# Full attention: heads paired on two halves of the partitions, scores issued a step ahead, maximum chunks set between halves of the value matmuls

## What is computed

```python
scores = jnp.einsum('bhtd,bhsd->bhts', q, k) * scale
attn = jax.nn.softmax(scores.astype(jnp.float32), axis=-1).astype(q.dtype)
y = jnp.einsum('bhts,bhsd->bhtd', attn, v)
```

## Time and profile before

| | |
|---|---|
| median of 3 runs | 7337.34 us (7335.41 to 7339.68) |
| the profiled execution's own time | 7338.15 us |
| its span | 7336.3 us |
| PE / PEld / DVE / ACT / POOL busy | 75 / 43 / 63 / 45 / 36 % of the span |
| maxima chunks reduced (L340) | 1904, from 130.2 to 2612.3 us of the span |
| exponentials (L517) | 896, 796.0 us |

### The profile page before, as it was taken

How to read it: one execution, slowest core, us unless ns; L and a number is a source line. 1 busy time by engine, 2 the same in 40 slices (tenths; PEclk the granted TensorE clock), 3 DMA queues, 4 the chain that set the end, 5 groups by cost and what they waited for, 6 DMA issues and landing times. The chain is left out here.

```text
span 7336.3 us, 228324 instructions
## 1 busy us (share of the span) xinstructions
PE 5478.9 (75%) x94991; PEld 3176.4 (43%) x95226; DVE 4621.9 (63%) x9757; ACT 3311.9 (45%) x6753; POOL 2637.1 (36%) x2351
## 2 busy tenths in 40 slices
PE   5777877454777746888888888888888888888874
PEld 1222222112232214555555555555555555555552
DVE  5666666345555545676676666666666766666764
ACT  1444444121333313555555555555555555555542
POOL 0000000000000005555555555555555555655550
PEclk9999999576898967888888888888888888888885
DMA  3011010002111101001100110011001100110000
GB/s 95 14 20 20 13 20 14 26 0 84 27 20 26 20 8 52 23 23 29 32 23 23 29 32 23 23 29 32 23 23 31 34 23 23 31 29 23 23 19 18
DMA packets 99949, 197.56 MB, mean 27 GB/s; under 512 B 23616, under 2 KB 50048, under 8 KB 99328
## 3 DMA queue, kind: packets, MB, share of 16 engines
q1 hardware_dynamic: 94944, 195.44, 10.3%
q10 hardware_dynamic: 4896, 0.84, 0.1%
HBM read 67.45 MB, written 27.26 MB: 13 GB/s over the span
## 5 line engine op out<-in xcount | busy, mean ns | idle before, releaser
L340 DVE TENSOR_REDUCE a_mpart<-a_pm 128x1 f32<-128x512 f32 (+2 forms) x1904 | 1087.4, 628 | 511.9 <-PE a_pm L412 316.7
L517 ACT ACTIVATE a_probs<-a_ps 128x1024 f32<-128x1024 f32 (+3 forms) x896 | 796.0, 930 | 1123.5 <-PE a_ps L433 856.2
L1219 ACT ACTIVATE w_probs<-w_pa,w_nm,w_rqs 128x64 f32<-128x64 f32 x3072 | 971.2, 415 | 126.3 <-DVE w_nm L1367 124.4
L412 PE MATMUL a_pm<-a_KZ,a_QS 128*128 128x512 bf16 (+3 forms) x1869 | 665.1, 390 | 301.9 <-DVE a_mpart L340 187.7
L1212 ACT ACTIVATE w_sq<-w_pr 128x512 f32<-128x512 f32 x768 | 466.2, 607 | 898.4 <-DVE w_sinb L1355 898.4
L324 POOL COPY a_V<-a_vals 128x288 f32 x32 | 14.5, 452 | 1913.0 <-PE a_po L449 1911.7
L1141 PE MATMUL w_pr<-w_xc,w_w 128*128 128x256 f32 (+1 forms) x1152 | 455.6, 576 | 293.9 <-issue 293.9
L433 PE MATMUL a_ps<-a_QS,a_KS 128*128 128x512 bf16 (+3 forms) x1688 | 514.9, 379 | 140.9 <-DMA a_KS<-k_parts 118.1
L929 POOL TENSOR_TENSOR w_sinb<-w_sinb,w_tabk 128x512 f32<-128x512 f32 x384 | 488.4, 1272 | 283.8 <-DVE w_sinb L1355 283.8
L955 POOL TENSOR_TENSOR w_probs<-w_probs,w_rden 128x512 f32<-128x512 f32 x384 | 392.9, 1044 | 539.0 <-DVE w_rden L1377 539.0
L1355 DVE STREAM_SHUFFLE w_sinb<-w_pr 128x512 f32<-128x512 f32 x768 | 562.6, 733 | 0.0
(11 more groups left out here) (218 smaller groups left out, 10160.9 us busy)
## 6 DMA issues: line engine op xcount, KB each, us to landing
w_Vp<-w_V SPq DMA_DIRECT2D x192, 384.0 KB, 3.7
w_Vp<-w_V SPq DMA_DIRECT2D x192, 128.0 KB, 3.4
a_QS<-q_parts SPq DMA_DIRECT2D x136, 96.0 KB, 3.4
a_KZ<-k_parts SPq DMA_DIRECT2D x136, 96.0 KB, 3.6
a_KS<-k_parts SPq DMA_DIRECT2D x136, 96.0 KB, 3.7
q_parts<-a1p_part SPq DMA_DIRECT2D x48, 128.0 KB, 1.8
k_parts<-a1p_part SPq DMA_DIRECT2D x48, 128.0 KB, 1.8
q_parts<-a2p_part SPq DMA_DIRECT2D x48, 128.0 KB, 1.8
```

The source lines that it names most:

```text
L340: nc.vector.reduce_max(mpart[:, h, qt, kc:kc + 1], p_m[:, k % 2, 0:width], AX_X).then_inc(max_read, 1)
L412: mm = nc.tensor.matmul(out, QS[:, par, h, qt * P:(qt + 1) * P], KZ[:, par, h, kc * CH:kc * CH + width], start=True, stop=True)
L517: nc.scalar.activation(probs[:, s % 2, 2 * pair:2 * pair + 2, c0:CH], p_s[:, pair, :, c0:CH], ACT.Exp, scale=SM_SCALE).then_inc(exped, 1)
L1219: op = nc.scalar.activation(probs[:, g, t, c, :], s_of(g)[:, t, c, :], ACT.Exp, bias=nm[:, g, t, c:c + 1], scale=scale_of(g)[:, t, c:c + 1])
```

## The change

- `QS` and `KS` hold two heads on the two halves of the partitions: head e of a pair on partitions 64e to 64e+47, its maxima on rows 64e+48 to 64e+50. `KZ` is gone: a maximum chunk reads 48 rows only, and a score 64. Four loads of QS and four of KS per group remain; `rows_of` issues six DMAs of 16 rows.
- Fills: DVE zeroes the (now half as long) `QS`, sets all of `KS` to -1, and fills `osum` and `p_o` with 1.0. SP waits for three of these.
- `next_score` issues the scores of step s+1 during step s (at the group's end, of the next group's step 0). The wait for operands stands in step 0, after the first of them.
- `weigh` belongs to its own step, and in steps of full width is split in two halves of 256 columns, with chunks between (order: scores pair 0, two chunks, scores pair 1, a chunk, half, a chunk, half, the rest).
- The chunks are spread by their width over all steps but the last three (a1: 5 each and once 4; a2: 10, 4, 3, 1, 7, 7, 5, 6, 5).
- ACT does `keep_out` (between the two exponentials of step 0, for the group before, and of the step after the first half's end). `turn_out` stands at the end of steps 1 and ends[0]+1, `normalise` in steps 2 and ends[0]+2.
- `turn_maxima` stands after `weigh` of step NS-3; ACT's `rows_of` stands before the exponentials of step NS-2 (before: NS-1).
- The mask matmuls of a2 still use all 128 rows; those of a score pair now stand behind both of its score matmuls.
- POOL copies the values two groups ahead.

```diff
-        QS = sb("QS", [P, 2, GH, SEQ], BF16)
-        KS = sb("KS", [P, 2, GH, SEQ], BF16)
-        KZ = sb("KZ", [P, 2, GH, SEQ], BF16)
+        QS = sb("QS", [P, 2, PAIRED, SEQ], BF16)
+        KS = sb("KS", [P, 2, PAIRED, SEQ], BF16)
...
+        room = [CH - c0 for _, _, c0 in steps[:NS - 3]]
+        need = [width + 64 for *_, width in chunks]
...
                 def load(g, par):
-                    for h in range(GH):
-                        sp.dma_start(QS[0:KROWS, par, h, :], qg[g, :, h, :]).then_inc(operands, 16)
-                        sp.dma_start(KZ[0:KROWS, par, h, :], kg[g, :, h, :]).then_inc(operands, 16)
-                        sp.dma_start(KS[0:KROWS, par, h, :], kg[g, :, h, :]).then_inc(operands, 16)
+                    for hp in range(PAIRED):
+                        for e in range(2):
+                            r = slice(64 * e, 64 * e + KROWS)
+                            sp.dma_start(QS[r, par, hp, :], qg[g, :, 2 * hp + e, :]).then_inc(operands, 16)
+                            sp.dma_start(KS[r, par, hp, :], kg[g, :, 2 * hp + e, :]).then_inc(operands, 16)
...
                 nc.vector.memset(QS[:, :, :, :], 0.0).then_inc(zeroed, 1)
-                nc.vector.memset(KZ[:, :, :, :], 0.0).then_inc(zeroed, 1)
+                nc.vector.memset(KS[:, :, :, :], -1.0).then_inc(zeroed, 1)
                 nc.vector.memset(mpart[:, :, :, :], NEG).then_inc(zeroed, 1)
-                dve.wait_ge(zeroed, 4 + FIRST)
-                nc.vector.memset(KS[32:64, :, :, :], -1.0).then_inc(zeroed, 1)
-                dve.wait_ge(zeroed, 5 + FIRST)
+                nc.vector.memset(osum[:, :], 1.0)
+                nc.vector.memset(p_o[:, :], 1.0).then_inc(ones_set, 1)
...
-                    mm = nc.tensor.matmul(out, QS[:, par, h, qt * P:(qt + 1) * P],
-                                          KZ[:, par, h, kc * CH:kc * CH + width], start=True, stop=True)
+                    r = slice(64 * e, 64 * e + KROWS)
+                    mm = nc.tensor.matmul(p_m[:, k % 2, 0:width], QS[r, par, hp, qt * P:(qt + 1) * P],
+                                          KS[r, par, hp, kc * CH:kc * CH + width], start=True, stop=True)
...
+                def next_score(s, g, par, pair):
+                    pe.wait_ge(exped, g * (2 * NS) + (2 * s + pair + 1) + FIRST)
+                    if s < NS - 1:
+                        score(s + 1, g, par, pair)
+                    else:
+                        if pair == 0:
+                            pe.wait_ge(m_stored, (g + 2) * 96)
+                        score(0, g + 1, 1 - par, pair)
...
+                            todo = list(range(first_chunk[s], first_chunk[s + 1]))
+                            parts = 2 if steps[s][2] == 0 else 1
+                            next_score(s, g, par, 0)
+                            if s == 0:
+                                pe.wait_ge(operands, (g + 2) * (2 * GH * 16))
+                            for k in todo[0:2]:
+                                max_chunk(k, g + 1, 1 - par)
+                            next_score(s, g, par, 1)
+                            for k in todo[2:3]:
+                                max_chunk(k, g + 1, 1 - par)
+                            weigh(s, g, par, 0, parts)
+                            for k in todo[3:4]:
+                                max_chunk(k, g + 1, 1 - par)
+                            if parts == 2:
+                                weigh(s, g, par, 1, parts)
+                            for k in todo[4:]:
+                                max_chunk(k, g + 1, 1 - par)
+                            if s == 1:
+                                turn_out(g * 2 - 1, g + 1)
+                            if s == ends[0] + 1:
+                                turn_out(g * 2, g + 1)
+                            if s == NS - 3:
+                                turn_maxima(g + 1)
...
-                            if s == NS - 1:
+                            if s == NS - 2:
                                 rows_of(1 - par, g + 1)
```

More of the change, by code:

```diff
@@ L278, in attention @@
         NS, NC = len(steps), len(chunks)
         ends = [s for s in range(NS) if s == NS - 1 or steps[s + 1][0] != steps[s][0]]
-        per_step = -(-NC // (NS - 3))
-        operands, stage_ready = sem("operands", 0), sem("stage_ready")
+        room = [CH - c0 for _, _, c0 in steps[:NS - 3]]
+        need = [width + 64 for *_, width in chunks]
+        first_chunk, done, k = [0], 0, 0
+        for s in range(NS - 3):
+            while k < NC and (done + need[k] / 2) * sum(room) <= sum(need) * sum(room[:s + 1]):
+                done += need[k]
+                k += 1
+            first_chunk.append(k if s < NS - 4 else NC)
@@ L426, in score @@
                     hq, kt, c0 = steps[s]
-                    pe.wait_ge(exped, (g * (2 * NS) + (2 * s + pair - 1 if s else 0)) + FIRST)
+                    q0 = hq * CH + c0
+                    diag = causal and kt * P >= hq * CH
                     for e in range(2):
-                        h = 2 * pair + e
-                        q0 = hq * CH + c0
-                        diag = causal and kt * P >= hq * CH
-                        mm = nc.tensor.matmul(p_s[:, pair, e, c0:CH], KS[:, par, h, kt * P:(kt + 1) * P],
-                                              QS[:, par, h, q0:(hq + 1) * CH], start=True, stop=True)
-                        if diag:
+                        r = slice(64 * e, 64 * e + 64)
+                        mm = nc.tensor.matmul(p_s[:, pair, e, c0:CH], KS[r, par, pair, kt * P:(kt + 1) * P],
+                                              QS[r, par, pair, q0:(hq + 1) * CH], start=True, stop=True)
+                    if diag:
+                        for e in range(2):
                             mm = nc.tensor.matmul(p_s[:, pair, e, c0:c0 + P], cmaskb[:, 0, :],
@@ L468, in _ @@
                 nc.tensor.transpose(rows0, mcol[:, :], ident[:, :]).then_inc(m_turned, 1)
-                with pe.Fori(0, GROUPS // 2) as i:
+                pe.wait_ge(m_stored, 96)
+                for pair in range(PAIRED):
+                    score(0, 0, 0, pair)
+                with nc.Fori(0, GROUPS // 2, engines=bass.OrderedEngineSet([pe.engine]), hint_back_edge=True) as i:
                     for par in range(2):
                         g = i * 2 + par
-                        pe.wait_ge(m_stored, g * 48 + 48)
-                        pe.wait_ge(operands, (g + 2) * (3 * GH * 16))
-                        k = 0
@@ L485, in _ @@
                             if s == NS - 3:
                                 turn_maxima(g + 1)
[L487 to L492 removed]
+                turn_out(GROUPS * 2 - 1, GROUPS + 1)
             @block.scalar
@@ L509, in _ @@
                             hq, kt, c0 = steps[s]
-                            if s == NS - 1:
+                            if s == NS - 2:
                                 rows_of(1 - par, g + 1)
-                            for pair in range(2):
+                            for pair in range(PAIRED):
+                                if pair == 1 and s == 0:
+                                    keep_out(g * 2 - 1, g * NS)
+                                if pair == 1 and s == ends[0] + 1:
+                                    keep_out(g * 2, g * NS + ends[0] + 1)
                                 act.wait_ge(scores, g * (2 * NS) + 2 * s + pair + 1 + FIRST)
                                 if pair == 0:
-                                    act.wait_ge(weighted, g * NS + max(s - 1, 0) + FIRST)
+                                    act.wait_ge(weighted, g * NS + s + FIRST)
                                 nc.scalar.activation(probs[:, s % 2, 2 * pair:2 * pair + 2, c0:CH],
```

140 lines of the change are left out of this document (68 added, 72 removed).

## The result

The changed kernel takes **7755.49 us** (median of 4 runs, 7739.55 to 7830.98) against 7338.51 for the kernel before on the same chip: ratio **1.0586** (95% interval 1.0553 to 1.0619). The forecast was 7296, its range ended at 7440. The profiled execution took 7754.07, with a span of 7752.2.

A forecast was written before the change was run, and what follows sets the result against it. With no engine full (PE 75%), a chain of waits was taken to set the time. Terms -30 - 5 - 36 + 45 - 31 + 8 + 3 + 5 = -41 us gave about 7296 us, range 7120 to 7440.

The forecast's parts named there:

- Prices, from the rows: Costs read from the earlier trace: a chunk 0.21 us of PE, its reduction possible after 0.41, DVE starting one every 0.60.
- Exit of a short shape, 0.13: On PE, leaving a 64-row array shape costs 0.13 us, with 0.35 as upper end and nothing as lower.
- Rival 2: Each shape exit on PE drains, 0.35 us instead of 0.13: a1's step 4.00, about 7588 us; chance 0.17.
- rival 1: PE's slots fit and DVE alone bounds: a1's step 3.0 us, about 7106 us in all; chance 0.22.
- Heads together: Scores of two heads on the array's two halves run side by side on PE, 0.22 us for both.
- Rival 4: Heads do not run together: 25 us more in a1 and 25 in a2, 7346 us, no change; chance 0.11.
- a1's steps, -30: a1's 13 steps with chunks: a step 3.56 us instead of 4.12, -1.9 us a group, -30 for 16.
- a1's switch, -5: Between groups of a1, last reduction to next group's first takes 16.8 us against 17.15: 15 times, -5 us.
- rival 3: Operand loads don't get shorter, being bound by their landing: +78 us, 7374 us in all; chance 0.05.
- a2, switch -36: Between groups of a2, last reduction to next group's first takes 16.0 us against 18.45: 15 times, -36 us.
- a2, steps +45: a2's steps with chunks grow from 32.8 to about 35.6 us a group: +45 us, called the least certain term.
- Starts, -31: Shorter fills and first loads at the start of each attention: -15.5 us each, -31 us together.

The follow-up runs named there:

- e3_before_short_rows: Kernel before, its order, loads and fills kept, with chunks reading only rows 0 to 47 and scores rows 0 to 63: 8280.36 us, ratio 1.1283.
- e7_rows_on_sp: New order, 128-row tiles, loads on three semaphores; SP issues maxima's DMAs, last value set precedes next group's scores, maxima turned earlier: 7087.84 us, ratio 0.9664.
- e72_rows_72: New order on the old 128-row tiles, but chunks and scores read rows 0 to 71: 7789.26 and 7822.31 us (ratio 1.0631), once 8160.02.
- e96_rows_96: New order on the old 128-row tiles, but chunks and scores read rows 0 to 95: 7351.13 us, ratio 1.0024.
- e1_order_full_rows: Changed kernel's order alone, on the old separate 128-row tiles with twelve loads, three DMAs of maxima and old fills: 7347.22 us, ratio 1.0012.
- e4_order_short_rows: New order on the old tiles, with chunks reading only rows 0 to 47 and scores rows 0 to 63: 8267.80 us, ratio 1.1270.

## Why the prediction was wrong

**The step that failed** stands in "Prices, from the rows": every PE duration (a chunk 0.21 us of PE, a value half 0.55, two scores 0.22 together) came from rows at the upper level of the clock (0.95 in a1's middle, 1.00 from 1120 to 1126), and was applied to matmuls of another height as if the clock were a given. The sum had no term for it, and none of the four rivals either. What the runs showed in its place: with the short matmuls the clock fell to 0.67 and 0.59, and a chunk at the lower level reaches the next one after 1.55 us in place of 0.90. The exit of a 64-row shape was bounded ("0.35 is kept as the upper end, nothing as the lower"), but the height's other effect was not bounded. The earlier trace rows had matmuls of 64 and 32 rows, taken for their exits alone. And the earlier trace rows had shown two scores at 1.03 us behind a wait, against 0.59 elsewhere (granted clock 0.50 from 248 to 251); the prediction priced that as slowness after idle time, and didn't ask when it ends. Short matmuls in place of 128-row ones cost 941 us in `before`'s own order (8280 against 7340), more than twenty times the gain that was forecast.

The busy share of PE doesn't tell the two levels apart. The kernel with short matmuls is busy 632 us of a1's 700 at a clock of 0.52; the kernel above whose maxima are written by SP, with 128 rows, is busy just as long (628 us) at 1.00, and its chunks last 387 ns in the mean:

```profile
300.00:1000.00 700.00, 628.34 (x4646) 204.89 (x4645) 520.53 (x869) 389.87 (x404) 4.99 (x11) 1.00 0.11 21
```

**Point by point.**

- *Exit of a short shape, 0.13:* a little less. From chunk to value half 0.31, of which the columns are 0.21: 0.10, as much as the known change from 128 rows. At the lower level a masked chunk of a2 reaches its mask after 0.54, of which 0.43 are its 512 columns (in the kernel before with short matmuls two scores last 1.03 at that level and one matmul 0.60), so 0.11:

```profile
2007.34 0.61 PE L412 MATMUL a_pm<-a_KS,a_QS 48*128 48x512 bf16 x1
2007.88 0.29 PE L415 MATMUL a_pm<-a_cmaskb 128*128 128x128 bf16 x1
```

  Rival 2 (0.35, a step of 4.00) is refuted, and rival 1 (a step of 3.0) too, by the 3.55 at the upper level.
- *Heads together:* yes. No row of before shows two matmuls of 64 rows and 512 columns side by side, which the 0.22 for two scores and the 3.1 of a2 assume; in the changed kernel both last 0.39 at the upper level, and the next chunk starts 0.23 behind them (593.68), where two of 128 rows last 0.59. Rival 4 falls.
- *a1's steps, -30:* 0.89 from chunk to chunk and 3.55 a step at the upper level, as forecast, and 3.61 a step in the order alone, with the heads one after the other. (The phase's parts add up to 49.6, not 49.8.) At the clock that it had, a1 took +170 instead.
- *a1's switch, -5:* up to the loads every sub-step came within 0.2, the loads were shorter still (6.0 against 6.8; rival 3 falls): the gap came out at 15.8 in the switch shown, 1 us below. What was accepted without a price of the alternative was the place of the DMAs; moving the three of the order alone gave 4 to 5 us a group.
- *a2, switch -36:* right, 16.3 in the mean against the forecast's 16.0.
- *a2, steps +45:* the step's cost can't be told from the clock's here. But the order alone, where no mask changes the height and no heads run together, tests a part of the term: without the 9.2 for exits and the 3.1 for heads, its other items make the phase some 3 us shorter (2.5 - 2.8 - 3), and it came out 2.1 longer (32.7 to 34.8). So what the order does in a2's steps was mis-sized too; by which item stays open.
- *Starts, -31:* -17.4 in a1; from a1's last maxima to a2's first, -12.9: near the forecast.
- *The order:* it was credited with most of a1's gain; alone it gives 1.0012. In a1 the phase with chunks does gain 1.6 us a group, and the switch takes 1.0 back.

Shown: short matmuls lower PE's clock level whatever the order (a chunk of a1's middle lasts 608 ns in the mean in the old order and 620 in the new, with 128 rows 402 and 397), and the layout alone loses as much as the changed kernel (1.0578 against 1.0586), though spread otherwise over a1 and a2. Open: why one group of a1 kept the upper level, why the order moves the loss from a2 to a1, and what about a short matmul lowers the clock. No experiment separated the 48 rows of the chunks from the 64 of the scores at equal numbers.

## What to carry to other kernels

Cutting padding rows from a matmul didn't shorten it here (0.39 us for a chunk of 48 rows at the upper level and for one of 128), and it took the granted clock from 0.95 to 0.67 in a1's middle and from 0.88 to 0.59 in a2; before reducing the rows of the matmuls that carry a kernel, time one build with nothing but the slices shortened. Make PE's clock a term of every sum: the durations of this profile hold only at the level at which they were read (a chunk of 48 rows lasts 0.39 at a clock of 1.00, 0.60 at 0.50). And where a group's end is a chain (maxima, DMAs, exponentials, scores, loads), ask of each link what stands behind it in its queue: moving one DMA issue by a step was worth 2.3%, where the reordering of every step had been worth nothing.

## What was not expected of the hardware

Clocks, busy shares and mean durations are those of a1's middle, 300 to 1000 us, in the run named.

- PE was busy 90% at a granted clock of 0.52 with matmuls of 48 and 64 rows (`e3_before_short_rows`), and 90% at 1.00 with 128 rows (`e7_rows_on_sp`). With 72 rows it was 92% and 0.57 (`e72_rows_72`), with 96 rows 82% and 0.92 (`e96_rows_96`), with 128 rows in the same order 80% and 0.94 (`e1_order_full_rows`).
- Rows 72 to 95 of `QS` are zeros. With them in the chunks and scores the clock was 0.92 and a chunk lasted 396 ns in the mean (`e96_rows_96`), without them 0.57 and 584 ns (`e72_rows_72`).
- The granted clock read 1.00 where the chunks lasted 620 ns in the mean (`e4_order_short_rows`); it also read 1.00 where they lasted 387 ns (`e7_rows_on_sp`).
- From a chunk of 48 rows to a matmul of another shape, 0.10 us passed beyond the chunk's columns at the upper level and 0.11 at the lower (`after`, the rows at 591.66 and 2007.34). The change from full to 32 columns took 0.10 before.
